# A four-layer vision tower on one core: gathers ahead of scatters in layer 0, shared-expert units in another order, and one-hots and softmax scalings divided between VectorE and ScalarE

## The reference, cut to what matters

```python
# L0 feed-forward: 16 experts, 2 per token, width 384, and a shared expert
topk_p, topk_i = jax.lax.top_k(softmax(xf @ w_gate + expert_bias), 2)
routed = routed + comb[:, e:e+1] * (silu(x @ wg[e]) * (x @ wu[e]) @ wd[e])   # for each e
# L2 feed-forward: 128 experts, 6 per token, at most 192 tokens each, width 464, shared expert of width 928
topk_idx = jax.lax.top_k(sig + e_bias, 6)[1]
out = routed + silu(x @ Wsg) * (x @ Wsu) @ Wsd
# L3 attention: 12 heads of 16, keys kept: the int(0.4 * 36) = 14 highest of a row
kth = jax.lax.top_k(attn_weights, top_k)[0][..., -1:]
attn = softmax(where(attn_weights >= kth, attn_weights, min_val))
```

## Time and profile before

| | us |
|---|---|
| median of 3 runs | 918.87 (918.73 to 923.22) |
| the profiled execution | 916.05, its span 914.0 |
| PE busy | 819.4 (90%) |
| PEld busy | 666.5 (73%) |
| DVE busy | 396.1 (43%) |
| ACT busy | 301.2 (33%) |
| POOL busy | 283.8 (31%) |

### The profile page before, as it was taken

How to read it: one execution, slowest core, us unless ns; L and a number is a source line. 1 busy time by engine, 2 the same in 40 slices (tenths; PEclk the granted TensorE clock), 3 DMA queues, 4 the chain that set the end, 5 groups by cost and what they waited for, 6 DMA issues and landing times. The chain is left out here.

```text
span 914.0 us, 18262 instructions
## 1 busy us (share of the span) xinstructions
PE 819.4 (90%) x6193; PEld 666.5 (73%) x6193; DVE 396.1 (43%) x1182; ACT 301.2 (33%) x630; POOL 283.8 (31%) x317
## 2 busy tenths in 40 slices
PE   8996988899989989999889999999999868898991
PEld 5775888675676569997558999999566656698990
DVE  1344222333551378884652222222153965454543
ACT  2430222325462276762301222222334123333340
POOL 0003554100011147760123444444110000357671
PEclk9988999997899889998879999999999877889995
DMA  9714898200000332200346899989841302478885
GB/s 362 274 29 158 278 289 267 68 1 1 1 1 1 146 99 71 73 21 1 108 161 208 299 316 305 327 290 306 246 125 54 114 3 73 136 218 271 264 259 148
DMA packets 55338, 145.56 MB, mean 159 GB/s; under 512 B 7776, under 2 KB 18736, under 8 KB 54768
## 3 DMA queue, kind: packets, MB, share of 16 engines
q1 hardware_dynamic: 46432, 122.44, 40.0%
q0 software_dynamic: 8848, 22.37, 8.9%
HBM read 131.51 MB, written 13.27 MB: 158 GB/s over the span
## 5 line engine op out<-in xcount | busy, mean ns | idle before, releaser
L1478 POOL DMA_INDIRECT L_xr<-x_rows_L,L_rows_in x89 | 89.8, 1010 | 40.6 <-issue 20.1
L2281 DVE TENSOR_TENSOR L_act<-L_hid,bank 116x512 f32<-116x512 f32 (+1 forms) x54 | 34.7, 643 | 151.7 <-ACT L_hid L2250 151.7
L2171 POOL DMA_INDIRECT y_rows_L<-L_yb,L_rows_out x54 | 53.9, 997 | 102.4 <-ACT L_yb L2256 95.6
L2250 ACT ACTIVATE L_hid<-bank 116x512 f32<-116x512 f32 (+1 forms) x54 | 30.3, 561 | 157.7 <-PE bank L2220 157.7
L2214 PE MATMUL bank<-L_xtb,L_w 128*116 128x128 f32 (+1 forms) x428 | 52.9, 277 | 0.0
L2214 PEld LDWEIGHTS bank<-L_xtb,L_w 128*116 128x116 f32 (+1 forms) x428 | 50.5, 186 | 0.0
L1544 POOL TENSOR_TENSOR L_s_up<-L_s_hid,L_s_up 116x288 f32<-116x288 f32 (+1 forms) x10 | 8.2, 816 | 115.8 <-ACT L_s_up L1538 115.8
L2214 PE MATMUL bank<-L_xtb,L_more 128*116 128x128 f32 (+1 forms) x364 | 44.1, 274 | 0.0
L1377 POOL TENSOR_TENSOR ssm_w_low<-ssm_wbc,ssm_w_high 128x512 fp32r<-128x512 f32 x24 | 30.9, 1292 | 41.4 <-ACT ssm_w_high L1332 41.4
L2214 PEld LDWEIGHTS bank<-L_xtb,L_more 128*116 128x116 f32 (+1 forms) x364 | 42.2, 184 | 0.0
L2230 PE MATMUL bank<-L_w,L_act 116*128 116x192 f32 (+1 forms) x214 | 42.1, 339 | 0.0
(11 more groups left out here) (460 smaller groups left out, 1868.0 us busy)
## 6 DMA issues: line engine op xcount, KB each, us to landing
L_w<-in_L2w SPq DMA_DIRECT2D x20, 696.0 KB, 5.0
L_more<-in_L2w SPq DMA_DIRECT2D x20, 696.0 KB, 5.5
L_w<-in_L2w SPq DMA_DIRECT2D x20, 384.0 KB, 6.3
L_more<-in_L2w SPq DMA_DIRECT2D x20, 384.0 KB, 7.1
L_w<-in_L0w SPq DMA_DIRECT2D x12, 576.0 KB, 3.9
ssm_wbc<-in_wBC SPq DMA_DIRECT2D x24, 256.0 KB, 2.7
L_w<-in_L3w SPq DMA_DIRECT2D x16, 384.0 KB, 3.0
L_more<-in_L0w SPq DMA_DIRECT2D x9, 576.0 KB, 3.9
```

Of the source, the lines that this page charges most:

```text
L1478: pool.indirect_dma_start(self.xr[j][:, :], None, self.x_rows[:, :], bass.IndirectOffsetOnAxis(ap=at, axis=0))\
L2171: pool.indirect_dma_start(X.y_rows[:, :], bass.IndirectOffsetOnAxis(ap=rows_out[h][:, j:j + 1], axis=0), y[s + j][:, :], None).then_inc(st ...
L2250: act.activation(hid[j][:, :, :], cols(gate_bank[(s + j) % 2][0:N, 0:C * R], C), ACT.Silu).then_inc(acted, 1)
L2281: dve.tensor_tensor(act_out[j][:, :, :], hid[j][:, :, :], cols(up_bank[(s + j) % 2][0:N, 0:C * R], C), ALU.mult)\
```

## The change

In the expert steps of layer 0 all three gathers of the next step stand ahead of the first scatter. In the routing of layer 2, two of six shared units move from ahead of the count to behind the plan, and ACT writes the last two of the six block one-hots of each tile: as relu(v - v * |block - base|), which is v where the two are equal and 0 elsewhere, `apart` holding the distance and `v` the token's code. In the attention of layer 3, for batches 0 and 1, ACT subtracts the maximum as the bias of 16 exponentials of 36 columns, in place of DVE's one subtraction, and scales by the inverted sum in 16 copies, in place of DVE's one product. `early` is 2 there and 0 elsewhere, where the code stays as it was.

```diff
-    "L2": dict(experts=128, top=6, ..., between=(6, 0, 2, 2), by_tile=(0, 2)),
+    "L2": dict(experts=128, top=6, ..., between=(4, 0, 2, 4), by_tile=(0, 2)),
...
         def turn(g):
-            pe.wait_ge(probs, g + 1)
+            if g < early:
+                pe.wait_ge(act_probs, g + 1)
+            else:
+                pe.wait_ge(probs, g + 1 - early)
...
         def exponentials(g):
             act.wait_ge(lowered, g + 1)
-            part = sc[:, CH * g:CH * g + CH, :]
-            act.activation(part, part, ACT.Exp).then_inc(exps, 1)
+            if g < early:
+                for i in range(CH * g, CH * g + CH):
+                    ins = act.activation(sc[:, i, :], sc[:, i, :], ACT.Exp, bias=mx[:, i:i + 1])
+            else:
+                part = sc[:, CH * g:CH * g + CH, :]
+                ins = act.activation(part, part, ACT.Exp)
+            ins.then_inc(exps, 1)
+
+        def scale(g):
+            if g < early:
+                act.wait_ge(inverted, g + 1)
+                for i in range(CH * g, CH * g + CH):
+                    ins = act.activation(sc[:, i, :], sc[:, i, :], ACT.Copy, scale=total[:, i:i + 1])
+                ins.then_inc(act_probs, 1)
 
         def take_turned(g):
+            scale(g)
...
+                if g < early:
+                    link(dve.tensor_scalar(top, top8[:, CH * g:CH * g + CH, 0], -1.0, None, ALU.mult))
+                else:
+                    link(dve.tensor_copy(top, top8[:, CH * g:CH * g + CH, 0]))
...
-            dve.tensor_tensor(part, part, spread(top, 2, SEQ), ALU.subtract).then_inc(lowered, 1)
+            if g < early:
+                dve.sem_inc(lowered, 1)
+            else:
+                dve.tensor_tensor(part, part, spread(top, 2, SEQ), ALU.subtract).then_inc(lowered, 1)
...
+            if g < early:
+                dve.reciprocal(tot, tot).then_inc(inverted, 1)
+                return
...
         for i in range(TILES):
             pe.wait_ge(paired, i + 1)
+            if by_act < K:
+                pe.wait_ge(act_paired, i + 1)
...
+        def pair_blocks(i):
+
+            if i >= 2:
+                act.wait_ge(pairs_used, i - 1)
+            vtok, minus = cols(p["vtok"], TILES), cols(minus_v[:, :], TILES)
+            if i:
+                act.wait_ge(act_paired, i)
+            for k in range(by_act, K):
+                ins = act.activation(apart[:, k - by_act, :], T.iota_bf[0:TILE, 0:B], ACT.Abs, bias=base[:, i, k:k + 1], scale=-1.0)
+            ins.then_inc(apart_in, 1)
+            act.wait_ge(apart_in, i + 2)
+            for k in range(by_act, K):
+                ins = act.activation(at_block[i % 2][:, k, :], apart[:, k - by_act, :], ACT.Relu, bias=vtok[:, i, k:k + 1],
+                                     scale=minus[:, i, k:k + 1])
+            ins.then_inc(act_paired, 1)
+
+        def between_units(u):
+            if u == 10:
+                act.wait_ge(base_known, 1)
+                for i in range(4):
+                    pair_blocks(i)
+            elif u == 12:
+                for i in range(4, TILES):
+                    pair_blocks(i)
...
-            for k in range(K):
+            for k in range(by_act):
                 ins = dve.tensor_scalar(at_block[i % 2][:, k, :], T.iota_bf[0:TILE, 0:B], base[:, i, k:k + 1],
...
                 fetch(0)
                 fetch(1)
+                if STEP == 3:
+                    fetch(2)
                 pool.wait_ge(stored[h], r * (16 * STEP) + 16)
                 pool.tensor_copy(rows_out[h][:, :], X.idx[:, bass.ds(q * STEP, STEP), 1]).then_inc(out_known, 1)
                 pool.wait_ge(out_known, q + 1)
                 put(0)
                 for j in range(2, STEP):
-                    fetch(j)
+                    if STEP > 3:
+                        fetch(j)
                     put(j - 1)
                 put(STEP - 1)
```

More of the change, by code:

```diff
@@ L49 @@
     "L0": dict(experts=16, top=2, pairs=2, cap=TOKENS, width=384, chunks=3, step=3, group=4, between=(2, 0, 2, 2), by_tile=(0,)),
-    "L2": dict(experts=128, top=6, pairs=6, cap=192, width=464, chunks=4, step=4, group=5, between=(6, 0, 2, 2), by_tile=(0, 2)),
+    "L2": dict(experts=128, top=6, pairs=6, cap=192, width=464, chunks=4, step=4, group=5, between=(4, 0, 2, 4), by_tile=(0, 2)),
     "L3": dict(experts=16, top=3, pairs=3, cap=TOKENS, width=384, chunks=3, step=4, group=4),
@@ L566, in head_attention @@
     pt = sb("pt", [128, IMAGES, 2, H3, SEQ]) if space is None else space[1]
+    early = BATCHES - 2 if sparse else 0
+    inverted, act_probs = sem("inverted"), sem("act_probs")
     scored, sc_in, lowered, exps, probs, turned, cleared, pt_in, pv, att_in, step = map(
@@ L719, in lower @@
                 link(ins)
-                link(dve.tensor_copy(top, top8[:, CH * g:CH * g + CH, 0]))
+                if g < early:
+                    link(dve.tensor_scalar(top, top8[:, CH * g:CH * g + CH, 0], -1.0, None, ALU.mult))
+                else:
+                    link(dve.tensor_copy(top, top8[:, CH * g:CH * g + CH, 0]))
                 link(dve.tensor_tensor(kept[:, CH * g:CH * g + CH, :], part,
@@ L1524, in second, with take @@
             mm.then_inc(self.down, 1)
-    def take(self, act, s, bank):
+    def take(self, act, s, bank, before_unit=None):
         if s:
@@ L1529, in take @@
         for u in range(2 * self.C):
+            if before_unit:
+                before_unit(u)
             v = self.C * s + u // 2
@@ L1803, in route @@
     at_block = [sb(f"at_block{i}", [TILE, K, B], BF16) for i in range(2)]
+    by_act = K - 2 if key == "L2" else K
+    if by_act < K:
+        apart = sb("apart", [TILE, 2, B], BF16)
+        minus_v = sb("minus_v", [TILE, TILES * 8])
     code, spare, y_row = sb("code", [R, B]), sb("spare", [R, B]), sb("y_row", [R, B])
@@ L1947, in _ @@
             act.activation(value[:, :, :], marked[:, :, :], ACT.Exp).then_inc(valued, 1)
-        if shared:
+        def pair_blocks(i):
[20 more added lines that the diff above has]
+                    pair_blocks(i)
+        if by_act < K:
+            act.activation(minus_v[:, :], p["vtok"], ACT.Copy, scale=-1.0).then_inc(apart_in, 1)
+            shared.take(act, 0, 4, between_units)
+        elif shared:
             shared.take(act, 0, 4)
@@ L2044, in _ @@
         link(dve.tensor_tensor(base[:, :, :], slot8[:, :, :], pos[:, :, :], ALU.subtract))
+        dve.sem_inc(base_known, 1)
         vtok = cols(p["vtok"], TILES)
```

4 lines of the change are left out of this document (2 added, 2 removed).

## The result

The changed kernel takes 915.68 us (median of 16 runs, 910.67 to 920.63); the kernel before, on the same chips, 922.78 (16 runs). The ratio is 0.994, 95% interval 0.9918 to 0.9962, a gain of 5.5 us by the ratio. The forecast was 906.6 against 918.87, a ratio of 0.9866, with a range of 901.5 to 912.5: the direction was right and the size was not, since under half of the 12.3 us came. The changed kernel was measured twice more beside experiments (ratios 0.9909 and 0.9897). The profiled execution has a span of 912.8 us, where before it was 914.0.

A forecast was written before the change was run, and what follows sets the result against it. TensorE, busy nine tenths of the span, was taken to bound the kernel, so gains lay in its waits. Terms of -5.9, -2.9 and -3.5 sum to -12.3 us, taking the median from 918.87 to 906.6 us, range 901.5 to 912.5.

The forecast's parts named there:

- Of 6.9 us I leave 1.0 for that: -5.9 us.: Layer 0's expert steps: earlier third gathers remove the 6.9 us of waits, less 1.0 for slower landings, gaining 5.9 us.
- landings may grow: Layer 0's gathers: DMA share rises from 82% to 90%, so landings may lengthen; 1.0 us was left for it.
- no DMA wait before the third block: Sign of being right in layer 0: no DMA wait at L2198 before a step's third block, steps of 10.9 us.
- Rival B: Layer 0's wait only moves: gathers land 1 us later, half the gain is left, 909.5 us; chance 0.14.
- so its first tile is ready at 454.2: Layer 2's routing: ScalarE first takes units 8 and 9, then has its first one-hot tile at 454.2 us.
- 1.5 us a tile: Layer 2's routing: ScalarE's four operations of 164 columns, 0.36 us each, take 1.5 us a tile with hand-overs.
- rival C: ScalarE's small operations in routing and attention do not overlap, a tile taking 1.8 us; 910.1 us in all, chance 0.12.
- I take 0.5 of it: Layer 2's second products (L1522): a low clock costs 2.2 us there, of which 0.5 was counted as gain.
- One of 36 columns: 0.25 us: Layer 3's attention: one ScalarE exponential of 36 columns costs 0.25 us, 16 of them 4.0 us.
- Nothing to spare: Layer 3's attention: exponentials(3) end at 740.0 us and VectorE wants them at 739.9, the narrowest place.
- rival E: Whole kernel within 0.5% of before: B and C together plus badly falling low clock stretches, 914.5 to 918 us; chance 0.07.

The follow-up runs named there:

- Edit 1: Layer 0's third gather issued ahead of the scatters; alone against the kernel before, 913.34 us, ratio 0.9979.
- e7: The kernel before without the weight loads in the last steps of layers 0 and 2, where no next step comes: 918.01 us, ratio 0.9993.
- e8: The changed kernel without the weight loads in the last steps of layers 0 and 2: 910.45 us, ratio 0.9899.
- e11: The kernel before with the gathers ahead of the scatters and without the loads of the last step: 913.12 us, ratio 0.9896.
- e14: The changed kernel without ScalarE's one-hots and without the loads of the last steps: 904.7 us, ratio 0.9873.
- Edits 2 and 3: Layer 2's routing with shared units reordered and two of six one-hots on ScalarE; alone against the kernel before, 910.08 us, ratio 0.9944.
- e9: The kernel before with layer 0's gate and up weights left at those of its first two steps, output not the reference's: 932.47 us, ratio 1.0102.
- e10: The kernel before with the gathers ahead of the scatters and the same layer 0 weights left out as in e9: 930.56 us, ratio 1.012.
- e13: The kernel before with ScalarE's one-hots alone, shared units in the old order: 912.64 us, ratio 0.9953.
- edit 2: Two of layer 2's six shared units moved from ahead of the count to behind the plan; alone against the kernel before, 913.71 us, ratio 0.9978.
- edit 3: ScalarE writes two of six block one-hots in layer 2's routing; alone against the kernel before, 912.64 us, ratio 0.9953.
- e2: The kernel before with the new order of the shared units alone, all six one-hots on VectorE: 913.71 us, ratio 0.9978.
- e12: The changed kernel with all six block one-hots on VectorE again: 911.27 us, ratio 0.9869.
- e4: The kernel before with the attention change of layer 3 alone: 913.88 us, ratio 0.9972.
- e6: The changed kernel without the gathers ahead of the scatters: 909.57 us, ratio 0.9904.
- Edit 4: Layer 3's attention with scaling on ScalarE in two of four batches; alone against the kernel before, 913.88 us, ratio 0.9972.
- e15: The changed kernel measured a third time, unchanged, beside e13 and e14: 906.86 us, ratio 0.9897.
- e5: The changed kernel measured once more, unchanged: 911.32 us, ratio 0.9909.

## Why the prediction was wrong, step by step

**Edit 1, the failed step.** "Of 6.9 us I leave 1.0 for that: -5.9 us." Over the five traces with the gathers ahead and the last loads in place, and the six without either edit, the waits fell from 5.8 to 1.8 us on average. The way to the last turning fell from 73.8 to 70.2: 3.6 us of the 5.9 forecast. The wait was not 6.9 to begin with: that one execution had the highest of six, 4.2 to 6.9. Then the tail takes back 1.9 of it, as the landing grows from 3.8 to 5.7 us, which leaves 1.7 at DVE's first sum (84.7 and 83.0). What is left at L279 is 92.1 - 90.9 = 1.2 us, with 3 to 5 us between traces of one kind and, in two of the five new ones, a low stretch behind the last turning. I had written that "landings may grow" and priced it inside the loop alone; I didn't follow the last scatter to the fetch that waits for it. e7, e8, e11 and e14 show the cause: without the 2.6 MB that nobody reads, the landing is 2.4 us in all four, and the gathers are worth 90.9 (e7) - 87.5 (mean of the three) = 3.4 us at L279. Why the same loads cost more with the new order shows in the four us behind the last scatter's issue: 298 to 409 GB/s move in the five traces with the gathers ahead, 169 to 222 in the six without, 62 or 63 in the four without the loads. The loop ends sooner, and the last scatter meets more of the loads. The sign "no DMA wait before the third block" did not come true (1.09 us at 111.32). Rival B had the size of the gain in the loop (half of it is left), not the place.

The Trainium skill (DMA: Bandwidth & Descriptors, Issuing engines are not separate DMA queues) says that transfers issued by SyncE and by GpSimd end up on the same 16 engines and interleave there. The landing of GpSimd's scatter agrees: 5.5 us with SP's loads, 2.4 without.

**Edits 2 and 3: -2.9 forecast, -4.3 measured, and the mechanism half wrong.** Five traces without either edit need 40.1 us on average from mask to first turning (38.4 to 41.2; e9 and e10, with other routing, left out), the six that have both 35.8. The step "so its first tile is ready at 454.2" is right to 0.1 us (453.25 + 0.94 = 454.19). But this first tile is also what PE's first pairing waits for, with the units moved or not (e13), so that edit 2 is worth nothing beside edit 3. Alone it brings that pairing to 11.1 and 11.6 us behind the mask (e2, e12), where both have 12.4 to 13.3, and these two traces beat both edits by 1.0 us. The third trace with it alone (e14, 37.7) does not: 11.2 us are at the low level there, and over the three the mean is 35.8, as with both edits. "1.5 us a tile" was 1.76 (452.46 to 454.22), close to the 1.8 of rival C. Over the same traces the last pairing ends 1.4 us sooner (25.1 to 23.7 behind the mask), not 2.4; the second products start 2.4 us sooner (29.2 to 26.8), as forecast, and take 8.03 us instead of 9.9. That last 1.9, for which "I take 0.5 of it" stands, is the gain above the forecast and goes with the clock; e4 has it without either edit. Without either edit 6.8 to 13.7 us of this stage run at the low level, with both 3.4 (6.8 in e6).

The Trainium skill (ScalarE: Activation LUTs, Rules for kernel authors) would have relu-like work on VectorE. The runs side with it here: 1.76 us for two one-hots on ScalarE, 1.47 for six on VectorE in the earlier trace rows.

**Edit 4: -3.5 forecast, -3.7 measured.** Eight traces with it average 39.5 us (38.8 to 40.4), seven without 43.2 (43.0 to 43.3). "One of 36 columns: 0.25 us" was 0.22; the third turning stands 36.2 us behind the first MAX8 instead of 39.0, 2.8 sooner as forecast. "Nothing to spare" was right: in the changed kernel's trace ACT ends exponentials(3) 0.08 us ahead of DVE's use (738.37 + 0.68 and 739.13), and in three of the eight (e4, e12, e15) DVE waits 0.4 to 0.7 us for them.

The Trainium skill (ScalarE: Activation LUTs, Rules for kernel authors) has a budget per ACTIVATE that gives, as an estimate, 0.33 us for 36 columns and 0.44 for 164. The trace agrees for how long a single one lasts (0.31 us on average for 36 columns, 0.43 for an Abs and 0.52 for a Relu of 164), but they overlap: one follows the other after 3.55 / 16 = 0.22 us, and after (0.76 + 0.94) / 4 = 0.43. Rival C, that they do not overlap, falls for the 36 columns.

**The sum.** In their places the edits are worth 1.2 + 4.3 + 3.7 = 9.2 us. The three measurements of the whole give 0.6, 0.9 and 1.0% of the time, 5.5, 8.4 and 9.4 us. The first one, which the forecast is held against, is 3.7 us short of 9.2. Its profiled execution lost 3.7 us between layer 1's norm and the next one, which no edit touches; of the changed kernel's other two traces one lost 1.5 there and one nothing, and over the 15 traces on the reference's data that distance is 24.3 to 28.1. Whether such stretches fill the gap of all 16 runs the traces can't say, since each run has only its mean clock (0.918 over them, 0.922 in e5). That remains open. That e15 took 906.86 us beside a forecast of 906.6 is no confirmation, since the kernel before took 915.03 there. The range left out rival E, in whose band the 915.68 lies though not for E's reason, and took the terms of one execution as if they were the kernel's.

## What to carry to other kernels

Follow a transfer past the loop in which you free it: the last one of a kind meets whatever prefetch the loop issues for a step that never comes, and such loads cost just where the tail has nothing to hide them. When two edits serve the same wait, work out each alone: here one engine's first result set the time with either order. Judge a change of a few us in its own stage and over several traces; layer 0's wait of 6.9 us was 4.2 to 6.9 in six traces with the same code there, and a stage that nobody touched took 24.3 to 28.1.

## What was not expected of the hardware

- The same PE work between two norms took 24.3 us at a granted clock of 1.00 and 28.1 at 0.85, in a stage with the same code and the same data.
- The scatter issued last by GpSimd needed 5.2 to 6.1 us until the fetch behind it could start while SP's 2.6 MB were under way (3.0 to 4.6 with the old order of gathers and scatters), and 2.4 us in all six traces without them or with a third of them.
- Sixteen ScalarE operations of 36 columns with a pointer bias or scale follow each other at 0.22 us, though each lasts 0.31; of 164 bf16 columns two Abs take 0.76, two Relu with both pointers 0.94.
